# Expert stage of a routed feed-forward kernel: 64 row spans in class order, with an accumulator for classes that begin inside one

## The reference, cut to what matters

```python
x = x + conv_attention(ln(x))              # 32 images of 16 x 16 pixels, 64 channels
xf = ln(x).reshape(8192, 64)               # tokens
top_w, top_i = top_k(xf @ Wg + bg, 2)      # 8 experts, 2 for each token
top_w = softmax(top_w)
for e in range(8):                         # w_dense is 0 for experts that were not picked
    h = gelu(xf @ W1[e] + b1[e])           # 64 -> 256
    out = out + w_dense[:, e] * (h @ W2[e] + b2[e])
x = x + out
```

## Time and profile before

| | us |
|---|---|
| median of 3 runs | 449.91 (448.43 to 450.3) |
| the profiled execution | 447.42 |
| its span, first to last instruction | 445.6 |
| PE busy in the span | 382.6 (86%) |
| DVE busy | 363.4 (82%) |
| POOL busy | 305.8 (69%) |
| ACT busy | 284.1 (64%) |

### The profile page before, as it was taken

How to read it: one execution, slowest core, us unless ns; L and a number is a source line. 1 busy time by engine, 2 the same in 40 slices (tenths; PEclk the granted TensorE clock), 3 DMA queues, 4 the chain that set the end, 5 groups by cost and what they waited for, 6 DMA issues and landing times.

```text
span 445.6 us, 15478 instructions
## 1 busy us (share of the span) xinstructions
PE 382.6 (86%) x5559; PEld 241.8 (54%) x5559; DVE 363.4 (82%) x1249; ACT 284.1 (64%) x616; POOL 305.8 (69%) x392
## 2 busy tenths in 40 slices
PE   8898978999999989899899789798879988988920
PEld 8345444455554444445444344334879877877920
DVE  4678989977798898898998999898887888888520
ACT  2466686789878878778778675433646655655610
POOL 4233447675846788888887866575777777777776
PEclk9999999999999999999999989969999999999975
DMA  9915900000000000000000000013433333233200
GB/s 220 252 33 188 217 1 1 0 2 1 2 1 2 13 20 14 19 20 20 14 26 14 20 31 26 26 43 87 107 88 84 74 69 69 61 84 77 68 25 0
DMA packets 35395, 23.65 MB, mean 53 GB/s; under 512 B 13632, under 2 KB 32815, under 8 KB 35064
## 3 DMA queue, kind: packets, MB, share of 16 engines
q1 hardware_dynamic: 29480, 15.75, 15.0%
q0 software_dynamic: 4960, 6.45, 4.6%
q10 hardware_dynamic: 880, 0.48, 0.6%
HBM read 14.11 MB, written 9.27 MB: 52 GB/s over the span
## 4 chain that ended last, share of the span: by engine, by line
PE 35%; DVE 29%; issue 15%; ACT 9%; POOL 8%; DVEq 2%; ACTq 0%; POOLq 0%
PE bank L1480 7%; PE bank L1401 5%; DVE bt L1294 3%; DVE mx L1171 3%; PE bank L1522 3%; POOL out L671 3%; PE bank L1509 3%; PE bank L1670 2%; DVE rowb L1148 2%; PE bank L1498 2%; PE bank L1653 2%; POOL pn L654 2%; DVE sm L1179 2%; DVE bt L1297 2%; ACT pt L805 2%
## 5 line engine op out<-in xcount | busy, mean ns | idle before, releaser
L654 POOL TENSOR_TENSOR pn<-pe_,rs 128x512 f32<-128x512 f32 x64 | 67.4, 1053 | 68.1 <-DVE rs L1182 67.8
L873 ACT ACTIVATE aa<-bank 128x512 f32<-128x512 f32 x91 | 54.4, 597 | 47.0 <-PE bank L1653 46.0
L1480 PE MATMUL bank<-aa,bd 64*64 64x256 f32 x512 | 70.1, 390 | 11.9 <-ACT pt L805 8.3
L630 POOL DMA_INDIRECT rows_hbm<-rowb,posu x64 | 64.7, 1011 | 22.4 <-issue 15.3
L671 POOL DMA_INDIRECT out<-bt,zs x63 | 62.7, 994 | 19.2 <-issue 15.5
L1483 PE MATMUL bank<-pt,bt 64*64 64x256 f32 x512 | 70.1, 391 | 0.0
L817 ACT ACTIVATE pe_<-sc 128x512 f32<-128x512 f32 x64 | 40.6, 634 | 40.9 <-DVE sc L1174 33.7
L1171 DVE TENSOR_REDUCE mx<-bank 128x8 f32<-128x512 f32 x64 | 43.8, 685 | 20.3 <-PE bank L1480 20.0
L1480 PEld LDWEIGHTS bank<-aa,bd 64*64 64x64 f32 x512 | 33.4, 132 | 45.3 <-issue 32.4
L1174 DVE TENSOR_TENSOR sc<-bank,mx 128x512 f32<-128x512 f32 x64 | 44.3, 692 | 2.2
L777 ACT COPY zs<-bank 128x512 f32<-128x512 f32 x64 | 37.1, 580 | 11.6 <-PE bank L1483 11.5
(11 more groups left out here) (287 smaller groups left out, 918.5 us busy)
## 6 DMA issues: line engine op xcount, KB each, us to landing
zs<-rows_hbm SPq DMA_DIRECT2D x91, 66.0 KB
wloc<-in_L_conv_w_local SPq DMA_DIRECT2D x2, 1152.0 KB, 9.0
...
rows_hbm<-rowb,posu POOLq DMA_INDIRECT x64
out<-bt,zs POOLq DMA_INDIRECT x63, 2.2
```

The costliest lines, as they stand in the source:

```text
L630: nc.gpsimd.indirect_dma_start(out=rows_hbm, out_offset=bass.IndirectOffsetOnAxis(ap=posu[:, t:t + 1], axis=0), in_=rowb[:, t], in_offset= ...
L654: nc.gpsimd.tensor_tensor(pn[:, v % 2, :].rearrange("p (h j) -> p h j", h=HEADS), pe_[:, v % 2], rs[:, v % 2].unsqueeze(2).broadcast_to([P ...
L873: nc.scalar.activation(hh[:, j % 2], hidb[j % 2][:].rearrange("p (q n) -> p q n", q=4), ACT.Gelu, scale=1.0 / (XS * WS)).then_inc(gelu_rea ...
L1480: scored = nc.tensor.matmul(dots[v % 2][same, w * 2 * P:(w + 1) * 2 * P], xq[same, t % 2, 2 * v + w], aa[same, t % 2, :, j0:j0 + WT], star ...
```

## The change

The full blocks after the 20 early ones and the 28 last ones are replaced by this:

- The rows that the early blocks have not taken, of all 28 classes in order, are cut into 44 spans of 128 without regard to where a class ends. 64 x 128 rows are all rows, so 20 + 44 = 64 blocks cover each row once, and each needs one scatter: 64 instead of 91.
- A span may hold the end of one class and the beginning of the next. It is computed with the experts of the class in which it starts. For the 27 classes 1 to 27 a seam block is computed ahead of the spans with the experts of that class: it loads 128 rows from so far ahead of the class's first row that row p of the block is row p of the span. Its result, weights times experts and, in column 64, the row's index, is added to the span's place in an accumulator `acc` (45 places of 65 numbers), times a mask `seam` that is 0 ahead of the class's first row (`seam_sum`). Seam blocks take the 27 places after the early ones and have no scatter.
- For a span, `begin` adds `acc` to the token and to the index, ahead of the two additions. For early blocks nothing changes there.
- What follows a class's last row must be zero, so that what the first class's experts make of it adds nothing. SP writes 28 blocks of 128 zero rows at the classes' ends (`zero_tails`), two behind each row load of blocks 6 to 19, and waits for all of them ahead of the load of block 20. Each class's area has 128 zeroed rows ahead of it (`SEG`).
- `acc` takes the place of ring records in `aa`, and the records in `rowb` go too: the ring has 15 instead of 28. ACT zeroes `acc` ahead of its first work of the expert stage.
- ACT takes over the copy of the second expert of blocks 7 to 19 (`take_second`). DVE's copies for blocks 20 to 34 lie among blocks 26 to 45, and for the rest 7/10 of a record follows each block from 47 on.
- The first table gets by with fewer steps, the second is made in six parts behind blocks 0, 2, 4, 19, 21 and 22.
- The index is also kept as a number (`IDX`) and made into a word by an addition (`oidx`); `mask` and `past` go. Two seam banks get one more small matmul.

The diff, cut:

```diff
+SEG = P + CAP
+DYN = NT
+BLOCKS = CLS - 1 + DYN
...
+SEAMS = CLS - 1
+MERGED = FIRST + SEAMS
...
-        SENT_FROM = RING - 10
+        acc = af[:, 2 * 4 * P:2 * 4 * P + (REST + 1) * (C + 1)].rearrange("p (b c) -> p b c", b=REST + 1)
...
+            def zero_tails(classes):
+
+                for c in classes:
+                    if c == 0:
+                        sp.wait_ge(fill_at, 1)
+                    if c % GANG == 0:
+                        tails[:] = values_of(sp, fillu[0:1, c:c + GANG], CLS * SEG)
+                    sp.dma_start(rows_hbm[bass.ds(tails[c % GANG], P), :], zrow[:]).then_inc(tails_zero, 16)
...
                 if k == 0:
-                    sp.wait_ge(last_ready, 1)
+                    sp.wait_ge(seam_at, 1)
+                    sp.wait_ge(tails_zero, 16 * CLS)
                     sp.wait_ge(sent[1], 16 * (NT - FIRST - CLS))
...
                 if j >= SLOTS:
                     i = j - SLOTS
-                    sp.wait_ge(stored[i % LANES], 16 * (i // LANES + 1))
+                    sp.wait_ge(comb_ready, i + 1)
+                    if i < FIRST:
+                        sp.wait_ge(stored[i % LANES], 16 * (i // LANES + 1))
                 start = starts[(d if d is not None and d < FIRST else k if d is None else d - FIRST) % GANG]
                 sp.dma_start(xr[:, j % SLOTS], rows_hbm[bass.ds(start, P), :]).then_inc(row_in[j % SLOTS], 16)
+                if FIRST - 14 <= j < FIRST:
+                    zero_tails(range(2 * (j - FIRST + 14), 2 * (j - FIRST + 15)))
...
-            for j in range(BLOCKS):
-                wait(pool, comb_ready, j + 1)
-                if full_of(j) is None:
-                    k = j - FIRST
-                    pool.wait_ge(masked, k + 1)
-                    idx_j = oidx[:, k:k + 1]
+            for o in range(DYN):
+                j = block_of(o)
+                if j < FIRST:
+                    pool.wait_ge(comb_ready, j + 1)
+                    idx_j = xr[:, j % SLOTS, IDXU:IDXU + 1].bitcast(U32)
                 else:
-                    idx_j = xr[:, j % SLOTS, 2 * C + 2:2 * C + 3].bitcast(U32)
+                    pool.wait_ge(comb_ready, j + 1)
...
+            act.wait_ge(dots_done, NT)
+            act.wait_ge(rows_set, 2)
+            nc.scalar.copy(acc, zrow[:, 0:C + 1].unsqueeze(1).broadcast_to([P, REST + 1, C + 1])).then_inc(acc_zero, 1)
...
+            def take_second(d):
+
+                if d % GANG == 0 or d == HEAD:
+                    begin = d - d % GANG
+                    second[:] = values_of(act, tbu[2:3, begin:begin + GANG], E - 1)
+                if d == HEAD:
+                    act.wait_ge(x1_ready, 2 * NG)
+                    act.wait_ge(att_done, NG)
+                    act.wait_ge(w1_ready, TG + 1)
+                if d >= RING:
+                    act.wait_ge(ffn2_done, block_of(d - RING) + 1)
+                nc.scalar.copy(wcur[d % RING][:, 1:2], wrec[:, bass.ds(second[d % GANG], 1)]).then_inc(second_ready, 1)
...
+                if j + HEAD < FIRST:
+                    take_second(j + HEAD)
...
-            def combine(j):
+            def first_sum(j):
 
                 row = xr[:, j % SLOTS]
-                wait(dve, ffn2_done, j + 1)
-                wait(dve, stored[j % LANES], 16 * (j // LANES))
-                nc.vector.scalar_tensor_tensor(ob[:, j % LANES], outb[j % 2][:, 0:C], row[:, 2 * C:2 * C + 1], row[:, C:2 * C],
-                                               ALU.mult, ALU.add).then_inc(comb_step, 1)
+                dve.wait_ge(ffn2_done, j + 1)
+                if j < FIRST:
+                    wait(dve, stored[j % LANES], 16 * (j // LANES))
+                    nc.vector.scalar_tensor_tensor(ob[:, j % LANES], outb[j % 2][:, 0:C], row[:, W0:W0 + 1], row[:, C:2 * C],
+                                                   ALU.mult, ALU.add).then_inc(comb_step, 1)
+                elif j < MERGED:
+                    wait(dve, acc_done, j - FIRST - 1)
+                    nc.vector.scalar_tensor_tensor(seamed[:, j % 2], outb[j % 2][:, C:2 * C + 1], row[:, W1:W1 + 1], row[:, C:2 * C + 1],
+                                                   ALU.mult, ALU.add).then_inc(comb_step, 1)
+                else:
+                    o = out_of(j)
+                    dve.wait_ge(begun, o - FIRST + 1)
+                    nc.vector.scalar_tensor_tensor(ob[:, o % LANES], outb[j % 2][:, 0:C], row[:, W0:W0 + 1], ob[:, o % LANES],
+                                                   ALU.mult, ALU.add).then_inc(comb_step, 1)
+
+            def second_sum(j):
+
+                row = xr[:, j % SLOTS]
                 dve.wait_ge(comb_step, j + 1)
-                nc.vector.scalar_tensor_tensor(ob[:, j % LANES], outb[j % 2][:, C:2 * C], row[:, 2 * C + 1:2 * C + 2], ob[:, j % LANES],
-                                               ALU.mult, ALU.add).then_inc(comb_ready, 1)
-
-            def mask(k):
-
-                j = FIRST + k
+                if FIRST <= j < MERGED:
+                    nc.vector.scalar_tensor_tensor(seamed[:, j % 2, 0:C], outb[j % 2][:, 0:C], row[:, W0:W0 + 1], seamed[:, j % 2, 0:C],
+                                                   ALU.mult, ALU.add).then_inc(comb_ready, 1)
+                else:
+                    o = out_of(j)
+                    nc.vector.scalar_tensor_tensor(ob[:, o % LANES], outb[j % 2][:, C:2 * C], row[:, W1:W1 + 1], ob[:, o % LANES],
+                                                   ALU.mult, ALU.add).then_inc(comb_ready, 1)
+
+            slots = [None] * GANG
+
+            def seam_sum(j):
+
+                k = j - FIRST
+                if k == 0:
+                    dve.wait_ge(acc_zero, 1)
+                    dve.wait_ge(slots_ready, 1)
+                    dve.wait_ge(route_step, rn[0])
+                if k % GANG == 0:
+                    slots[:GANG] = values_of(dve, tblu[0:1, 1, k + 1:min(k + 1 + GANG, CLS)], REST)
+                at_ = acc[:, bass.ds(slots[k % GANG], 1)].rearrange("p b c -> p (b c)")
+                dve.wait_ge(comb_ready, j + 1)
+                wait(dve, acc_done, k)
+                nc.vector.scalar_tensor_tensor(at_, seamed[:, j % 2], seam[:, k + 1:k + 2], at_, ALU.mult, ALU.add).then_inc(acc_done, 1)
+
+            def begin(j):
+
+                o = out_of(j)
+                row, b = xr[:, j % SLOTS], o - FIRST
                 dve.wait_ge(row_in[j % SLOTS], 16 * (j // SLOTS + 1))
-                nc.vector.scalar_tensor_tensor(oidx[:, k:k + 1], xr[:, j % SLOTS, 2 * C + 2:2 * C + 3].bitcast(U32), 2 * NOROW - 1,
-                                               past[:, k:k + 1], ALU.bitwise_and, ALU.bitwise_or).then_inc(masked, 1)
+                wait(dve, stored[o % LANES], 16 * (o // LANES))
+                if b == 0:
+                    dve.wait_ge(acc_done, SEAMS)
+                nc.vector.tensor_tensor(oidx[:, b:b + 1], row[:, IDX:IDX + 1], acc[:, b, C:C + 1], ALU.add)
+                nc.vector.tensor_tensor(ob[:, o % LANES], row[:, C:2 * C], acc[:, b, 0:C], ALU.add).then_inc(begun, 1)
 
             taken = 8
             while taken < 2 * HEAD:
                 take_weights(taken // 2, taken % 2)
                 taken += 1
+            taken = HEAD
             for j in range(BLOCKS):
-                combine(j)
-                if j == FIRST - 8:
-                    count_full(1)
-                if j == FIRST - 4:
-                    split_full(1)
-                    dve.wait_ge(route_step, rn[0])
-                if j == TABLE - 4:
-                    scan_full(tbl[:, 8])
-                if j == TABLE - 3:
-                    pick_class()
-                if j == TABLE - 2:
-                    place_blocks()
+                if j == MERGED:
+                    seam_sum(j - 1)
+                    begin(j)
+                first_sum(j)
+                if FIRST < j < MERGED:
+                    seam_sum(j - 1)
+                if MERGED <= j < BLOCKS - 1:
+                    begin(j + 1)
+                second_sum(j)
+                if j in (0, 2, 4):
+                    second_table(j // 2)
+                if j in (TABLE - 6, TABLE - 4, TABLE - 3):
+                    second_table({6: 3, 4: 4, 3: 5}[TABLE - j])
                 if j == TABLE:
                     read_table(1)
-                if full_of(j) is None:
-                    mask(j - FIRST)
-                ahead = min(2 * (j + 1 + HEAD), 2 * FIRST) if j < TABLE else 2 * FIRST + (j - TABLE + 1) * 7 // 4
-                while taken < 2 * DYN and taken < ahead:
-                    take_weights(taken // 2, taken % 2)
+                ahead = min(j + 1 + HEAD, FIRST) if j <= TABLE else FIRST + min(RING, (j - TABLE + 1) * 3 // 4)
+                if j >= MERGED:
+                    ahead = FIRST + RING + (j - MERGED + 1) * 7 // 10
+                while taken < min(ahead, DYN):
+                    take_weights(taken, 0)
+                    if taken >= FIRST:
+                        take_weights(taken, 1)
```

167 lines of the change are left out of this document (92 added, 75 removed).

## The result

The forecast was 443.8 us, 6 us faster. The changed kernel took **454.66 us** (median of 4, 452.92 to 456.57) beside 450.11 for the kernel before (448.43 to 451.93): a ratio of 1.012 [1.008, 1.016], some 5 us slower. Timed again with other runs it was 455.17 beside 449.05, 1.012 [1.007, 1.018]. The forecast had the wrong sign, and the range (434 to 454) missed by 0.7.

What follows compares the result with a forecast made beforehand. GpSimd's scatters, with VectorE behind them, were taken to bound the kernel. Block starts of 315.2, 348, 380 and 435.9 gave span 439.5, 6.1 us less; 449.91 - 6.1 = 443.8 us, range 434 to 454.

Steps and rivals of the forecast that it cites:

- The fill: ScalarE zeroing the accumulator of 2925 elements ahead of the first transposed rows: 2.6 us, all on the path to block 0.
- The drop of the clock: TensorE, idle before block 0, falls to half rate for about 3.5 us from about 313: 1.5 us lost, 0.5 counted.
- The chain to block 20: SyncE's twelve passes of 2.1 us from 314.0 to 339.2, then zeros landing and row load: block 20 starts at 348.
- The seams: Blocks 20 to 46, no scatters: VectorE's work sums to 31.5 us against TensorE's 27.8; taken as 32, block 47 at 380.
- The late stage: Blocks 47 to 90: VectorE 1.24 us a block, GpSimd 1.28 to 1.30, about equally late; block 90 at 435.9.
- the rivals: SyncE costing nothing 0.18; VectorE dearer 0.15; SyncE's queue jamming 0.11; copies and scatters excluding each other 0.03; clock staying low 0.03.
- SyncE's term: Block 20's start by SyncE's cost per DMA: 348 at 0.6 us, 344.4 at 0.5, 352.3 at 0.72, 366 at 1.1.
- the late block: Time per block from 47 to 90: 1.28 us, with bounds 1.18 to 1.48 by how the two new VectorE operations fit.
- the queue of scatters: At the kernel's end, 14 scatters one behind the other on GpSimd; removing them can give at most 15 us.

Runs made afterwards that it cites:

- x_fill: The changed kernel with the accumulator zeroed in five pieces in ScalarE's passes of blocks 13 to 17, not in one ahead of block 0: 453.09 us, ratio 1.011.
- b_zero: The kernel before with only the 28 zero transfers added (to a spare place) and the wait for them before block 20's load: 453.25 us, ratio 1.011.

## Why the forecast was wrong

The right parts first. Taking scatters off GpSimd frees it (64 of them, idle for 36 us). The fill was priced at 2.6 and takes 2.64. The drop of the clock came where I put it (0.50 from 313.7 to 320.6), though for twice as long. The early stage is SyncE's and not ScalarE's, with TensorE waiting for the row of block 20. The forecast for the last scatter was 435.9 + 0.7 = 436.6, and it came at 448.5. The mechanism was right. What failed are three terms of the sum, each too small, the largest of them SyncE's chain of issues. The 11.9 us between forecast and measurement, by these terms:

**The chain to block 20: 5.85 us.** Half of it is its start. I let the passes of blocks 6 and 7 run before TensorE starts and take nothing. But the first zero transfer needs the last row counts. These came at 312.63, the first zeros at 313.28, and the two passes filled SyncE's queue until 315.9. Then SyncE waited 0.6 us for TensorE to transpose the rows of block 2, and block 8's load went out at 316.95 instead of 314.0: 3.0 us. Of this the index conversion has 1.25, a new operation in the middle of the attention that my list of changes left out; the profiles' own scatter is as large. A pass was 2.2 and not 2.1 us, so the passes end at 343.4 where 339.2 was forecast, 1.2 more. From there to the load of block 20 it took 3.0 instead of 2.3: 1.9 for the zeros to land, and 1.05 for the read of four addresses and the issue, which I had left out. From the load to the sum it took 7.45 instead of 6.5 us. Here the forecast had no clock: TensorE waited 2.07 us for the row of block 19 and 1.43 for that of block 20, and the granted clock fell to 0.50 again (344.5 to 351.3). In seven profiles with two transfers a pass or more this stretch took 7.4 to 7.7 us where its mean clock was 0.77, 7.45 at 0.67 and 8.2 to 8.7 at 0.57 to 0.60, so I put about 1 us down to it; no run tests it by itself. Block 0, which I had 3.55 too early, enters with the 0.6 us above at most: x_fill moves it, and block 20 stays. (In the recorded sum 339.2 + 2.3 + 2.3 is 343.8 and not 344.0, and block 20 comes to 347.5; the 348 is rounded up.)

**The seams: 3.7 us.** I summed VectorE at 31.5 and took 32; it was busy for 27.6 and idle for 8.1, and the stage took 35.66. The groups of blocks 20 to 46 (count, busy us, mean ns, idle before):

```profile
L1378 DVE SCALAR_TENSOR_TENSOR aa<-bt,seam,aa 128x65 f32 x27 | 7.7, 284 | 4.3 <-issue 4.2 <-DVE bt L1357 0.2
L1344 DVE SCALAR_TENSOR_TENSOR bt<-bank,zs 128x65 f32<-128x65 f32 x27 | 7.6, 283 | 1.3 <-PE bank L1762 0.6 <-PE bank L1767 0.4 <-DVE tbu L1175 0.2
```

The seven register reads ahead of the accumulator's sums cost 4.2 us, where I had 2.8; the four pairs for the copies 2.1 (I had 2.2). TensorE and the table's result cost 1.3 us of waiting which a sum over VectorE alone does not hold. Busy time was 1.1 more (27.6 instead of 26.5), and the rest is gaps too small to have a cause in the view.

**The late stage: 2.4 us.** The forecast let VectorE and GpSimd be equally late at 1.28 us a block. VectorE was quicker (blocks 47 to 90 in 52.4 us, 1.22 each), GpSimd slower: 57.5 us for 43 steps, 1.337, against 1.276 to 1.30 in the earlier trace rows. So the last scatter starts 6.6 us behind block 90's first addition and not 0.7. The 10 long scatters have 2.1 us of the 2.6 by which 43 steps exceed 1.276. In the old late stage it was more the copies that waited: the groups of them took 0.38 to 0.50 us on the mean there, and 0.37 to 0.45 in the new one. Why the meeting turned from the copy's cost into the scatter's, no run shows.

**Why the sign turned.** None of the rivals is the case that happened. SyncE's term came out inside the bounds that I gave (353.85, between 352.3 and 366), and so did the late block, but every stage on the dear side, and each hands its lateness on. The gain was capped at 15 us by the queue of scatters, and b_zero shows what that queue was worth: it hid 6 of 10 us. The sum did let every late stage through to the end, so this is not the step that failed; but the forecast never says that the queue is cover as well as time to win. Its margin of 6 us stood on terms that together were 12 us off, though SyncE's and the late block's stayed inside their own bounds; the seams had been given none.

What stays open is what else, beside the conversion's 1.25 us, is in the 3.0 us at the chain's start: the counts move by more than that from profile to profile.
